# Query and key parts in DRAM by blocks of 512 tokens, loaded two batches at a time

## What is computed

```
q, k, v = proj(Wq), proj(Wk), proj(Wv)            # (batch, head, 256, 8)
first:   scores = q k^T / sqrt(8), causal          # layer 1
second:  scores = q k^T / sqrt(8), all keys        # layer 2, q and v with a LoRA term
out = softmax(scores) v ;  x = x + out Wo + bo
```

## Time and profile before

| | |
|---|---|
| three runs | 2057.14, 2054.34, 2055.64 us; median 2055.64 us |
| the profiled execution | 2063.16 us, of which the span of instructions is 2061.4 us |
| busy share of the span | PE 77%, DVE 63%, PE's weight loads 53%, ACT 51%, POOL 39% |
| first attention, first load issue to last scores | about 893 to 1385 us, with the experts from about 1040 to 1215 us |
| second attention | about 1434 to 1760 us, with the dense experts from about 1531 to 1608 us |
| mean DMA rate | 63 GB/s over the span |

### The profile page before, as it was taken

The page is one execution under the profiler, slowest core; times in us unless marked ns, Lnnn a source line. Parts: engine busy times, 40 slices in busy tenths (PEclk is TensorE's granted clock), DMA queues, the critical chain, the costliest instruction groups (busy, mean ns, idle before and its releaser), DMA issues. The chain is left out here.

```text
span 2061.4 us, 34299 instructions
## 1 busy us (share of the span) xinstructions
PE 1583.8 (77%) x12241; PEld 1089.1 (53%) x12242; DVE 1293.2 (63%) x2310; ACT 1056.0 (51%) x1921; POOL 796.1 (39%) x803
## 2 busy tenths in 40 slices
PE   6818688888887667641889999984589999739974
PEld 5605466666654444610667776652245444637863
DVE  7403787787888888751644457758753798624334
ACT  1205877887776666240544445554454677414421
POOL 1570655555679997275012233331500000060042
PEclk9959899999998998665899999997699999669997
DMA  5201111111000010571321125512641251211312
GB/s 154 80 28 36 55 49 50 34 44 53 28 25 26 26 32 11 213 211 40 61 59 58 59 59 82 82 26 82 126 75 59 33 70 27 88 53 35 99 52 56
DMA packets 153337, 130.58 MB, mean 63 GB/s; under 512 B 18929, under 2 KB 137865, under 8 KB 152915
## 3 DMA queue, kind: packets, MB, share of 16 engines
q1 hardware_dynamic: 140554, 104.54, 20.6%
q0 software_dynamic: 12544, 23.82, 4.2%
q10 hardware_dynamic: 72, 0.03, 0.0%
HBM read 77.08 MB, written 52.43 MB: 63 GB/s over the span
## 5 line engine op out<-in xcount | busy, mean ns | idle before, releaser
L740 POOL TENSOR_TENSOR xn_t<-xn_t,scan_du 128x512 f32<-128x512 f32 x256 | 320.7, 1270 | 158.1 <-ACT xn_t L885 104.8
L953 DVE TENSOR_TENSOR_SCAN xn_t<-banks,xn_t 128x512 f32<-128x512 f32 x256 | 311.8, 1218 | 73.5 <-ACT banks L875 43.2
L785 PE MATMUL banks<-scan_hc,ident 128*128 128x256 f32 x1024 | 295.7, 415 | 47.3 <-DVE scan_hc L959 47.2
L2383 ACT ACTIVATE att_pr<-banks 128x768 f32<-128x768 f32 (+1 forms) x256 | 234.2, 917 | 138.7 <-PE banks L2275 83.8
L875 ACT ACTIVATE banks<-delta,scan_exp_centre,a_neg 128x255 f32<-128x255 f32 x512 | 265.5, 560 | 15.6 <-DVE xn_t L953 15.2
L785 PEld LDWEIGHTS banks<-scan_hc,ident 128*128 128x128 f32 x1024 | 192.6, 206 | 107.6 <-DVE scan_hc L959 70.0
L959 DVE TENSOR_TENSOR scan_hc<-xn_t,banks 128x512 f32<-128x512 f32 x256 | 175.9, 687 | 39.4 <-PE banks L770 19.3
L2427 DVE TENSOR_REDUCE att_mb<-banks 128x6 f32<-128x768 f32 x128 | 121.8, 955 | 107.7 <-remote 63.7
L2242 PE MATMUL banks<-att_ks,att_qs 48*128 48x256 bf16 (+1 forms) x1024 | 113.3, 278 | 83.9 <-DMA att_ks<-k_parts 30.8
L2431 DVE TENSOR_REDUCE att_mb<-banks 128x4 f32<-128x1024 f32 x128 | 153.9, 1222 | 23.6 <-PE banks L2242 18.6
L1009 POOL DMA_INDIRECT disp<-xn_tok,places x128 | 136.2, 1064 | 71.9 <-issue 38.4
(11 more groups left out here) (386 smaller groups left out, 3357.6 us busy)
## 6 DMA issues: line engine op xcount, KB each, us to landing
scan_ew<-f_packed SPq DMA_DIRECT2D x12, 578.0 KB, 4.1
q_parts<-att_p_parts SPq DMA_DIRECT2D x16, 384.0 KB, 4.1
k_parts<-att_p_parts SPq DMA_DIRECT2D x16, 384.0 KB, 6.1
att_qs<-q_parts SPq DMA_DIRECT2D x64, 96.0 KB
att_ks<-k_parts SPq DMA_DIRECT2D x64, 96.0 KB
gau_ew<-f_packed SPq DMA_DIRECT2D x8, 578.0 KB
disp<-zeros SPq DMA_DIRECT2D x1, 4608.0 KB, 14.8
att_xin<-disp SPq DMA_DIRECT2D x72, 64.0 KB
```

Of the source, the lines that this page charges most:

```text
L740: nc.gpsimd.tensor_tensor(bu[:, i % RING], b_sb[:, q % 2], du[:, b % 2, c:c + 1, :].to_broadcast([P, 2, T]), ALU.mult).then_inc(s.bu_made, 1)
L785: ins = nc.tensor.matmul(bank(Y_BANK)[:, c, :], g.ident[:], hc[:, i % RING, n, :], start=False, stop=(i % (PAIRS * DC) == PAIRS * DC - 1 a ...
L953: v.tensor_tensor_scan(rows(h[:, i % 2]), g.ps[:, DA + i % RING, :], rows(bu[:, i % RING]), 0.0, ALU.mult, ALU.add).then_inc(s.scan_done, 1)
L2383: nc.scalar.activation(pr[:, i % RING], g.ps[:, at:at + 2, 0:W], ACT.Exp, scale=scale).then_inc(s.p_ready, 1)
```

## The change

The DRAM tensors of parts get the shape (8 chunks, 3 parts, 128 rows, 512 tokens), for both attentions. The 8 head pairs of one channel of one chunk then are 8 rows of 512 tokens that lie behind each other: one contiguous piece of 8 KB. A slot of `qs` and `ks` holds two batches; there are three slots in place of four. `load_half` loads one half of a chunk, again with 6 DMAs, each of the same partitions as before and of twice the bytes. The early loads fetch chunks 0 and 1 (four batches); then chunk 2 is loaded at once. Behind that a load is issued only in every second batch: after the scores of batch b = 1, 3, 5, 7, 9, for chunk b // 2 + 3. PE's matmuls read the same elements at other addresses.

```diff
-        qp = nc.dram_tensor("q1_parts", (3, D, N), BF16, kind="Internal").ap()
-        kp = nc.dram_tensor("k1_parts", (3, D, N), BF16, kind="Internal").ap()
+        qp = nc.dram_tensor("q1_parts", (N // 512, 3, D, 512), BF16, kind="Internal").ap()
+        kp = nc.dram_tensor("k1_parts", (N // 512, 3, D, 512), BF16, kind="Internal").ap()
...
             for m, out in ((0, q_parts), (1, k_parts)):
-                sp.dma_start(out[:, :, ch * CH:(ch + 1) * CH].rearrange("a r t -> r a t"),
+                sp.dma_start(out[ch].rearrange("a r t -> r a t"),
                              parts[:, ch % PB, 3 * m:3 * m + 3]).then_inc(stored[ch % PB], 16)
-            if ch == EARLY:
-                sp.wait_ge(stored[0], 32)
+            if ch in (EARLY, EARLY + 2):
+                sp.wait_ge(stored[ch // 2 - 1], 32)
             if EARLY <= ch < EARLY + 4:
                 early_load(sp, (ch - EARLY) // 2, (ch - EARLY) % 2)
...
-    BUFS = 4
+    BUFS = 3
...
-        qs = s.sb("qs", [P, BUFS, PAIRS, T], BF16)
-        ks = s.sb("ks", [P, BUFS, PAIRS, T], BF16)
+        qs = s.sb("qs", [P, BUFS, PAIRS, 2 * T], BF16)
+        ks = s.sb("ks", [P, BUFS, PAIRS, 2 * T], BF16)
...
-        def load_half(sp, b, half):
-            tok, p, at = slice(b * T, (b + 1) * T), b % BUFS, half * HR
+        def load_half(sp, c, half):
+            p, at = c % BUFS, half * HR
             for row, n in ((0, 3), (3, 2), (5, 1)):
-                sp.dma_start(qs[at + row * HD:at + (row + n) * HD, p], q_parts[
-                    0:n, :, tok].rearrange("a (d g j) t -> g (a d) j t", g=2, j=PAIRS)[half]).then_inc(qk_in[p], 16)
+                sp.dma_start(qs[at + row * HD:at + (row + n) * HD, p], q_parts[c, 0:n].rearrange(
+                    "a (d g j) t -> g (a d) j t", g=2, j=PAIRS)[half]).then_inc(qk_in[p], 16)
...
+        def slot(b):
+            return b // 2 % BUFS, b % 2 * T
...
-                eng.dma_start(qs[half * HR + KR:half * HR + KM, b % BUFS],
+                p, at = slot(b)
+                eng.dma_start(qs[half * HR + KR:half * HR + KM, p, :, at:at + T],
                               mt[half * 2 * PAIRS:(half + 1) * 2 * PAIRS, b % 2, :]).then_inc(mx_in[b % 2], 16)
...
                 parts.sync(sp)
                 load(2)
                 for b in range(BATCH - 1):
                     top(sp, b + 1)
-                    if b == 0:
-                        load(3)
                     if b == 1 and dense:
                         job.weights(sp)
-                    if b + BUFS < BATCH:
+                    if b % 2 == 1 and b // 2 + BUFS < NCH:
                         sp.wait_ge(s.s_ready, (b + 1) * PAIRS)
-                        load(b + BUFS)
+                        load(b // 2 + BUFS)
```

More of the change, by code:

```diff
@@ L2058, in attention @@
                   "f_y", "f_yt", "f_z", "f_zb", "f_zg", "f_added"]
-    with section(nc, title, *names, *PROJECT, "w_in", "filled", "ones_set", "consts", "biased", "qk_in0", "qk_in1", "qk_in2", "qk_in3",
+    with section(nc, title, *names, *PROJECT, "w_in", "filled", "ones_set", "consts", "biased", "qk_in0", "qk_in1", "qk_in2",
                  "mx_in0", "mx_in1", "m_ready", "m_taken", "m_step", "nm_ready", "turned_nm", "mt_ready",
@@ L2074, in attention @@
             ahead_q = s.sb("ahead_q", [P, 2, P], BF16)
[L2075 removed]
+        qk_in = (s.qk_in0, s.qk_in1, s.qk_in2)
         mx_in = (s.mx_in0, s.mx_in1)
@@ L2087, in weights, with early_load @@
                 sp.dma_start(dst[:], src).then_inc(s.w_in, 16)
-        def load_half(sp, b, half):
-            tok, p, at = slice(b * T, (b + 1) * T), b % BUFS, half * HR
+        def load_half(sp, c, half):
+            p, at = c % BUFS, half * HR
             for row, n in ((0, 3), (3, 2), (5, 1)):
-                sp.dma_start(qs[at + row * HD:at + (row + n) * HD, p], q_parts[
-                    0:n, :, tok].rearrange("a (d g j) t -> g (a d) j t", g=2, j=PAIRS)[half]).then_inc(qk_in[p], 16)
-                sp.dma_start(ks[at + row * HD:at + (row + n) * HD, p], k_parts[
-                    3 - n:3, :, tok].rearrange("a (d g j) t -> g (a d) j t", g=2, j=PAIRS)[half]).then_inc(qk_in[p], 16)
-        def early_load(sp, b, half):
+                sp.dma_start(qs[at + row * HD:at + (row + n) * HD, p], q_parts[c, 0:n].rearrange(
+                    "a (d g j) t -> g (a d) j t", g=2, j=PAIRS)[half]).then_inc(qk_in[p], 16)
+                sp.dma_start(ks[at + row * HD:at + (row + n) * HD, p], k_parts[c, 3 - n:3].rearrange(
+                    "a (d g j) t -> g (a d) j t", g=2, j=PAIRS)[half]).then_inc(qk_in[p], 16)
+        def early_load(sp, c, half):
             sp.wait_ge(s.filled, FILLS)
-            load_half(sp, b, half)
+            load_half(sp, c, half)
+        def slot(b):
+            return b // 2 % BUFS, b % 2 * T
         def fill(pool):
@@ L2181, in _, with load @@
             def _(sp):
-                def load(b):
-                    if b % 2 == 0:
-                        parts.chunk_stored(sp, b // 2)
+                def load(c):
+                    parts.chunk_stored(sp, c)
                     for half in range(2):
-                        load_half(sp, b, half)
+                        load_half(sp, c, half)
                 parts.sync(sp)
@@ L2230, in maximum @@
                     b, j = divmod(i, PAIRS)
-                    p, step = b % BUFS, i - LEAD
+                    (p, at), step = slot(b), i - LEAD
                     if j == 0:
-                        pe.wait_ge(qk_in[p], (b // BUFS + 1) * LOADS)
+                        pe.wait_ge(qk_in[p], (b // 2 // BUFS + 1) * LOADS)
                     if step >= 1:
@@ L2255, in scores @@
                     b, j = divmod(i, PAIRS)
-                    p = b % BUFS
+                    p, at = slot(b)
                     if j == 0:
@@ L2577, in attn2 @@
 def attn2(nc, g, t, m):
-    qp = nc.dram_tensor("q2_parts", (3, D, N), BF16, kind="Internal").ap()
-    kp = nc.dram_tensor("k2_parts", (3, D, N), BF16, kind="Internal").ap()
+    qp = nc.dram_tensor("q2_parts", (N // 512, 3, D, 512), BF16, kind="Internal").ap()
+    kp = nc.dram_tensor("k2_parts", (N // 512, 3, D, 512), BF16, kind="Internal").ap()
     def prologue(loads, fill):
```

6 lines of the change are left out of this document (4 added, 2 removed).

## The result

The changed kernel takes 2118.57 us (median of four runs, 2111.9 to 2120.62) against 2056.16 us of the kernel before (four runs): 62.4 us more, a ratio of 1.031 with the interval 1.0288 to 1.0333. The forecast was 2103 us, range 2042 to 2126, slower with a chance of 0.77. The profiled execution took 2118.91 us, so that it is a typical one, while that of before was 7.5 us above the median of the three runs known at the forecast; the two spans are 55.7 us apart.

What follows compares the result with a forecast made beforehand. PE was taken to bound both attentions' steady parts (busy 148.35 of 160 and 103.86 of 105 us). Terms summed to +47.5 us on the profiled 2063.16, giving 2110.7, or 2103 us as median; range 2042 to 2126.

Steps and rivals of the forecast that it cites:

- How long two batches take: A chunk's load takes 15.6 us, twice today's 7.8, because few partitions are written at a time; lower bound 3.8 us.
- The estimate from the ports: Load of a chunk: 16 SBUF ports at some 27 GB/s each give 14.5 us, whatever the piece size.
- Stalls in the second attention: Scores behind chunk loads issued at b = 5, 7, 9: late `top` costs 6.4 us each, 19.2 in all.
- the clock's part: After a PE stall the granted clock stays halved some 6 us: 2.7 us lost in second attention, 1.4 in first.
- Stalls in the first attention: Scores behind chunk loads issued at b = 5, 7, 9: late `top` costs 3.4 us each, 10.2 in all.
- Experts: First attention: third token tile, queued behind the load of chunk 4, makes PE wait 7.5 us longer than today's 3.21.
- Chunk 3: Its load at b = 1: old and new stalls cancel to 0 in first attention, +0.6 us in second.
- The stall at batch 2: First attention: PE's 3.60 us wait for `top` at 1010.91 would go with its clock loss, -5.0 us.
- that for the keys: Second attention: PE's 4.52 us wait at 1490.18 would go with its clock loss, -7.2 us.
- the one behind the dense weights: Second attention: PE's 4.71 us `top` stall at 1515.47 would grow by 7.8 us, its clock already lost.
- Starts: Doubled early loads delay both attentions' beginnings: second +8 us (5 for store and keys, 3 for `top(0)`), first +2.
- Faster: Rival: piece size bounds the loads, a chunk takes 3.8 us, stalls vanish: -29 us, 2027 us; chance 0.18.

Runs made afterwards that it cites:

- interleaved halves: Changed kernel with the 12 DMAs of a chunk issued in turn for rows 0 to 47 and 64 to 111; ratio 1.0119 to the kernel before.
- 48 partitions: Changed kernel with four DMAs of 48 partitions for a chunk in place of twelve, some rows holding wrong parts; ratio 1.0053 to the kernel before.
- the run with the halves apart: Changed kernel with each chunk's load issued in two halves behind consecutive batches, at most 768 KB ahead of a `top`; ratio 1.0026 to the kernel before.
- The run with the layout alone: Kernel before with only the new DRAM layout, loads of one batch in four slots as before; ratio 1.0007 to the kernel before.
- pieces of 1 KB: Changed kernel with the old DRAM layout, the same two-batch loads in 1 KB instead of 8 KB pieces; ratio 1.0388 to the kernel before.
- the interleaved kernel before: Kernel before with only the DMA order changed, rows 0 to 47 and 64 to 111 in turn; 2033.66 us, ratio 0.9902 to the kernel before.

## Why the prediction was right, and where its sizes were off

The case forecast was the one that came: slower, by `top` behind a load that is no quicker for its larger pieces. The time lies in the range, but the sum was 8 us short by the profiles, and 15 by the medians (62.4 against 47.5), the rest being the profiled execution of before that was slower than its kind. That it is 8 and not more is in part luck: an error of +8.9 in the first attention's stalls stands against one of -5.5 in its first batches.

*How long two batches take.* Right in the second attention: 16 us at 99 GB/s for the forecast 15.6. The runs with interleaved halves (12 us) and with 48 partitions (10 us) bear out the reason given, few partitions at a time, since neither changed the pieces, though the second changed the number of DMAs with the partitions. They do not tell whether it is the ports of the SBUF that bound it or how rows are shared out among the engines. The estimate from the ports that the Trainium skill gives (SBUF — State Buffer, "Door 1: The DMA port swizzle"), 14.5 us, was some 1.5 us short.

*Stalls in the second attention.* Forecast 3.7 + 2.7 us, three times 19.2; measured 4.74, 4.94 and 4.77 us, and 22.1 in all. That is 4.8 + 2.6 each, so the clock's part was right, and `top` is 1.1 us later by a load that is longer by half a microsecond and by its own time behind it: the scores start 1.3 to 1.7 us behind the load's last bytes, where the forecast put 1.1, a term for which it showed no row.

*Stalls in the first attention.* Forecast 10.2, measured 19.1: the largest error. The step that failed took 7.8 us a batch, read from one load in the second attention, for the first as well. In the trace of before, eight loads of one batch in the steady part of the first attention, beside POOL's gathers, take 8.2 to 9.1 us from first to last packet, 8.6 in the mean, and eight in the second 7.5 to 9.0, in the mean 8.1. Twice these means are 17.2 and 16.2 us; the loads of the change take 16.8 to 17.7 and 15.9 to 16.5. I should have read the rate where I used it, and from more than one load. This makes up some 1.8 of the 3 us by which each stall is too short. The rest: the scores start 1.6 us behind the load and not 1.1, and PE is ready about half a microsecond sooner than a batch of 14.15 us made it. The clock's part, 1.4 us a stall, was right. The row at 1266.79 shows another price inside the same stall: PE stood 3.09 us with nothing in the profile to wait for, and 1.22 for `top`.

*Experts.* Forecast 7.5, measured 8.0; the third tile waits 9.33 us where it was 3.21. With half of the load in that place, as in the run with the halves apart, the wait is 0.35.

*Chunk 3.* Forecast 0 and +0.6, measured -5.5 and -1.5. The stall at batch 2 and that for the keys went as forecast. In the first attention the new stall is 2.81 us, where 3.7 were forecast, and its clock falls into the next row of the table. Besides, the stall of 3.60 us in the trace of before had cost 2.5 us behind itself and not 1.4 (batch 2 takes 15.5 us there, 13.0 without a stall), a wait of 1.12 us for keys went too, and batch 0 is 1.0 us shorter. The run with the layout alone does not show the stall of 3.60 us and has 43.1 us in this stretch, so that some of the gain is one of this profiled execution of before. In the second attention the one behind the dense weights is 9.15 us, some 3 us short of the 4.71 + 7.8 foreseen.

*Starts.* +8.9 for +8, but by other parts: the store (last cast 27.4 us behind the first, not 23.0) and the first keys (7.5 us behind it, not 3.5) took 8.4 us and not 5, and `top(0)`, for which 3 were added, took 1.0 more (5.35 for 4.34) and was made good elsewhere. The first attention's +4.4 for +2 lies within its bounds.

*The rivals.* "Faster" asked for 12 us or less a chunk by the pieces alone; against pieces of 1 KB they give 1.3 us of 17.5, against 512 bytes nothing. Its sum was sound where the rate was had by other means: the stalls that it would have removed are those that the interleaved kernel before does remove, 20 us by the medians of that call for 29 forecast.

## What to carry to other kernels

Before making pieces larger, find out what bounds the transfer. Here the rate was 100 GB/s with pieces of 512 bytes and 99 with 8 KB, the engines were shown busy, and few partitions were written at a time; the order of the DMAs over distant partitions was then worth more than their pieces, and cost nothing. Count a small transfer that something waits for with all bytes issued ahead of it, on whichever queue: fewer and larger loads can cost more than many small ones, at the same rate. And read a rate in the stretch in which you use it.

## What the runs showed of the hardware

- DMAs of 24, 16 and 8 partitions to rows 0 to 47 and 64 to 111 partly overlap when issued in turn: 131 GB/s against 99 to 100, with pieces of 512 bytes and of 8 KB alike.
- PE's instructions seem to come late behind loads of data: in the first attention behind the experts, fetches of 16 KB that came at most 9.6 us apart in the kernel before came up to 13.6 us apart, and at these places PE stood up to 4.2 us with nothing in the profile to wait for.
- Two DMAs of 8 KB issued by ACT at 1388.25, with 2.35 MB of SP's two chunks still to move, ended at 1405.30, 17 us later, and 5.4 us ahead of these chunks; PE waited 16.61 us for them. With 1.5 MB in one load they ended together with it.
- The kernel before took 1878.8 us on one chip and 2047.8 to 2056.2 on others; the second attention's steady batches took 12.4 us in both of its profiles, at 1878.8 and at 2056.2 us.
